# Layer 2 up to its MLP on whole float32 weights, attended beside the choice of tokens

## What is computed

```
x = _layernorm(x + attention(x, Wq, Wk, Wv, Wo))        # band: |block_i - block_j| <= 2, blocks of 64
scores = x @ w_router;  idx = sort(top_k(scores, 128))   # for each batch
sel = x[b, idx];  h = rms_norm(sel, ln1_w)
q, k, v = h @ wq + bq, h @ wk + bk, h @ wv + bv          # then rotary on q and k
att = softmax(causal(q @ k.T / sqrt(128)))               # over the chosen tokens of both batches
x1 = sel + (att @ v) @ wo
processed = x1 + (silu(rms_norm(x1, ln2_w) @ w_gate) * (rms_norm(x1, ln2_w) @ w_up)) @ w_down
gated = sigmoid(sel_scores) * processed + (1 - sigmoid(sel_scores)) * sel
x = _layernorm(x + x.at[b, idx].set(gated))
```

## Time and profile before

| What | Value |
|---|---|
| Median of three runs | 1432.89 us (1432.02 to 1435.05) |
| The profiled execution's own time | 1435.52 us |
| Its span, first to last instruction | 1433.5 us |
| TensorE, VectorE, ScalarE, GpSimd busy | 1286.4, 905.2, 606.8, 313.4 us |
| Instructions in the span | 19759 |
| Mean granted clock of TensorE | 0.953 of 2.4 GHz |
| Moved by DMA | 89.61 MB |

### The profile page before, as it was taken

One profiled execution on the slowest core, in us unless ns is written; L12 is line 12 of the kernel. 1 busy time (PEld: TensorE's weight loads), 2 busy tenths in 40 slices (PEclk: granted clock), 3 DMA queues, 4 the chain that ended last, 5 costly groups with the idle time before them and its releaser, 6 DMA issues.

```text
span 1433.5 us, 19759 instructions
## 1 busy us (share of the span) xinstructions
PE 1286.4 (90%) x7624; PEld 1145.9 (80%) x7624; DVE 905.2 (63%) x2328; ACT 606.8 (42%) x1388; POOL 313.4 (22%) x221
## 2 busy tenths in 40 slices
PE   6999999999999999999999999999998733767795
PEld 5898989889898988877879898989886633666795
DVE  4556565665565565787866556565556787686465
ACT  4444444444444444333434444444444222435352
POOL 2101120202020111231211021111202462252374
PEclk9999999999999999999999999999998876798798
DMA  5100110101010110133101010101100443253262
GB/s 172 35 22 30 31 44 30 45 16 45 15 45 30 45 65 10 64 99 118 45 26 45 15 45 26 34 30 40 40 33 1 161 147 96 77 170 124 75 207 101
DMA packets 70846, 89.61 MB, mean 63 GB/s; under 512 B 3360, under 2 KB 52512, under 8 KB 70752
## 3 DMA queue, kind: packets, MB, share of 16 engines
q1 hardware_dynamic: 70336, 87.04, 18.7%
q0 software_dynamic: 416, 1.31, 0.3%
HBM read 79.43 MB, written 8.91 MB: 62 GB/s over the span
## 4 chain that ended last, share of the span: by engine, by line
PE 67%; DVE 21%; ACT 7%; issue 3%; DMA 1%; POOL 0%; SPq 0%; ACTq 0%; DVEq 0%; POOLq 0%
PE proj L759 33%; PE y L759 10%; PE s L759 9%; PE o L759 8%; DVE arena L1179 8%; ACT arena L1020 4%; PE tp L831 4%; ACT prob L1054 2%; DVE prob L1214 2%; DVE work L1296 2%; DVE work L1388 1%; DVE yacc L1248 1%; ACT prob L1126 1%; DVE bn_out L1261 1%; DVE work L1391 1%
## 5 line engine op out<-in xcount | busy, mean ns | idle before, releaser
L759 PE MATMUL proj<-arena 128*128 128x256 f32 (+1 forms) x3552 | 649.3, 334 | 11.7 <-DVE arena L1179 7.5
L759 PEld LDWEIGHTS proj<-arena 128*128 128x128 f32 x3552 | 547.6, 192 | 74.1 <-DVE arena L1179 9.6
L1509 POOL TENSOR_TENSOR arena<-wraw,arena 128x1024 fp32r<-128x1024 f32 x98 | 242.8, 2487 | 936.0 <-ACT arena L1020 936.0
L1054 ACT ACTIVATE prob<-prob,stat 128x384 f32<-128x384 f32 (+1 forms) x256 | 151.0, 590 | 499.6 <-DVE stat L1214 499.6
L1179 DVE TENSOR_TENSOR arena<-proj,arena 128x512 fp32r<-128x512 f32 (+1 forms) x282 | 159.1, 569 | 314.1 <-ACT arena L1020 312.8
L759 PE MATMUL o<-arena 128*128 128x256 f32 (+1 forms) x1248 | 255.1, 333 | 8.8 <-DVE arena L1179 5.8
L759 PE MATMUL s<-arena 128*128 128x384 f32 (+3 forms) x1008 | 224.4, 340 | 10.8 <-DVE arena L1179 10.8
L759 PE MATMUL y<-arena 128*128 128x512 f32 (+1 forms) x888 | 214.7, 379 | 8.4 <-DVE stat L1419 4.4
L759 PEld LDWEIGHTS s<-arena 128*128 128x128 f32 x1008 | 175.2, 195 | 30.8 <-DVE arena L1179 15.7
L759 PEld LDWEIGHTS o<-arena 128*128 128x128 f32 x1248 | 185.8, 199 | 15.0 <-DVE arena L1179 7.7
L1179 DVE TENSOR_TENSOR arena<-tp,arena 128x384 fp32r<-128x384 f32 (+2 forms) x273 | 142.4, 522 | 83.5 <-ACT arena L1020 83.0
(11 more groups left out here) (136 smaller groups left out, 565.2 us busy)
## 6 DMA issues: line engine op xcount, KB each, us to landing
wraw<-in_L_attn_Wq SPq DMA_DIRECT2D x16, 512.0 KB, 3.3
wraw<-in_L_attn_Wk SPq DMA_DIRECT2D x16, 512.0 KB, 3.3
wraw<-in_L_attn_Wv SPq DMA_DIRECT2D x16, 512.0 KB, 3.3
wraw<-in_L_attn_Wo SPq DMA_DIRECT2D x16, 512.0 KB, 3.7
wraw<-in_L_ffn_wq SPq DMA_DIRECT2D x16, 512.0 KB, 5.1
yacc<-in_L_attn_hidden_states SPq DMA_DIRECT2D x16, 256.0 KB, 3.0
y_dram<-yacc SPq DMA_DIRECT2D x16, 256.0 KB, 3.2
out<-work SPq DMA_DIRECT2D x16, 256.0 KB, 2.1
```

Source lines behind the costliest of these rows:

```text
L759: ins = e.matmul(out_ap, l[a], r[b], start=first and i == 0 and j == 0, stop=final and i == n - 1 and j == 2, skip_group_check=skip)
L1054: e.activation(prob[s][:, 0:n], prob[s][:, 0:n], ACT.Exp, bias=stat[:, 4 * s + 1:4 * s + 2], scale=-1.0, accum_out=stat[:, 4 * s + 2:4 * s ...
L1509: e.tensor_tensor(lo, wraw[n % RAW_SLOTS][:], hi.bitcast(F32), ALU.subtract).then_inc(*G_.inc("wsplit", n, "lo"))
```

## The change

- **Whole products.** From the normed rows of layer 2 to the product with wo there are no halves: `one_pass` multiplies float32 tiles as they are. Weights wq, wk, wv and wo go by DMA into eight "homes" of 512 KB in the space of layer 1's transposed input, and no engine splits them. ScalarE copies each result from PSUM once (`whole_copy`).
- **Bias.** The eight bias rows are loaded once, split into halves on 40 partitions, and added by one fast product of 512 columns a block (`unit_row`, `ub`).
- **Rotation.** Sine, cosine and sum are VectorE's, read from PSUM; GpSimd's part is gone. The scaling of probabilities and both norm rows move from VectorE to ScalarE, with `shift` computed on GpSimd.
- **Last head of layer 1.** Its output is split tile by tile (`ot`) and not in halves of 512, and its output projection begins three ticks earlier.
- **Ranking in quarters.** `rows`, `count` and `tie` run for two tiles at a time, as soon as these are normed; `rank` adds six columns of counts.
- **Order.** Steps of layer 2 are tagged; each tick runs them in the order of `FLOW`. A pair of heads starts when its q, k and v blocks are there, so pairs of batch 0 stand among the comparisons of batch 1. The product with wo, the residual and the norm are done for each batch by itself.
- **End.** The gate is applied before the MLP, and after the last product one step takes the place of four; both batches' roots come before both rows.

```diff
+        def one_pass(e, out_ap, pairs, first, final, skip=False):
+            n = len(pairs)
+            for i, (l, r) in enumerate(pairs):
+                ins = e.matmul(out_ap, l, r, start=first and i == 0, stop=final and i == n - 1, skip_group_check=skip)
...
-                    ins = three_passes(e, bank[to][:, half * GW:(half + 1) * GW],
-                                       [([hT[0][:, k, :], hT[1][:, k, :]], [w4[0][:, k, :], w4[1][:, k, :]])
-                                        for k in range(KT)], half == 0, half == 1, skip=True)
+                    pe.wait_ge(*landed("p2", b, n, half))
+                    ins = one_pass(e, to, [(hT[:, 2 * half + k, :], w2[:, k, :]) for k in range(2)], half == 0, False, skip=True)
                     if half == 1:
-                        ins.then_inc(*T_.inc("p2", b, n, "made"))
+                        pe.wait_ge(*V_.at("ubias", "lo"))
+                        row = BIAS_AT[which] + c
+                        ins = e.matmul(to, spread(unit_row[:, row:row + 1], P), ub, start=False, stop=True,
+                                       skip_group_check=True)
...
+                elif kind == "ubias":
+                    act.wait_ge(*T_.at("out", NB * NG - 2, TT - 1, "made"))
+                    act.wait_ge(*V_.at("ubias", "zero"))
+                    act.wait_ge(*bias_loaded.all())
+                    hi_part(ub, work[1][0:BIAS_ROWS, :], "ubias")
...
+                elif kind == "lnorm":
+                    act.wait_ge(*G_.at("ln", b, t, "shift"))
+                    e.activation(row, row, ACT.Identity, bias=shift[i][:], scale=rstd[i][:]).then_inc(*S_.inc("lnorm", b, t, "row"))
...
+                    act.wait_ge(*V_.at("an2", b, n, "recip"))
+                    for h in range(2):
+                        of_head = prob[s][:, h * nk:(h + 1) * nk]
+                        ins = e.activation(of_head, of_head, ACT.Copy, scale=rc[:, h:h + 1])
...
-            if 0 <= u - END < TT:
-                project_out(NB * NG - 1, u - END)
-                running.append(finish_layer1(NB - 1, u - END))
+            for t in range(TT):
+                if u == END - 4 + t and t < TT - 1:
+                    job("ot", t)
+                if u == END - 3 + min(t, TT - 2):
+                    project_out(NB * NG - 1, t)
+                    running.append([finish_layer1(NB - 1, t), None])
...
+        FLOW = {None: 0, "choose": 0.5, "res": 0.7, "resh": 0.8, "o2": 1, "av2": 2, "at2": 3, "an2": 4, "as2": 5, "p2t": 6,
+                "p2r": 7, "p2": 8}
+        def tick(*later):
+            for entry in sorted(running, key=lambda entry: FLOW[entry[1]]):
+                if entry[1] in later:
+                    continue
+                entry[1] = next(entry[0], running)
+                if entry[1] is running:
+                    running.remove(entry)
...
+            if front and not any(entry[1] == "p2" for entry in running) and front[0][0] in h_there:
+                begin(project2(*front.pop(0)))
...
+                    sp.wait_ge(*T_.at(*emptied_by[n]))
+                    src = homely[n][1]
+                    e.dma_start(home[home_of[n]].rearrange("p (k n) -> p k n", k=src.shape[1]), src
+                                ).then_inc(home_loaded[home_of[n]].sem, 16)
...
-                    after(e.tensor_tensor(x1, bank[f"s{b}"][:, :], x1, ALU.add), "fin", b, "mlp")
-                    after(e.tensor_scalar(x1, x1, g[:, 1:2], None, ALU.mult), "fin", b, "gated")
-                    after(e.scalar_tensor_tensor(x1, x_sel[b][:], g[:, 2:3], x1, ALU.mult, ALU.add), "fin", b, "mixed")
-                    after(e.tensor_tensor(x1, x1, x_sel[b][:], ALU.add), "fin", b, "sum")
-                    after(e.bn_stats(bn_out[b][:], x1), "fin", b, "stats")
+                    after(e.scalar_tensor_tensor(y1, bank[f"s{b}"][:, :], gate[:, 4 * b + 1:4 * b + 2], y1, ALU.mult, ALU.add),
+                          "fin", b, "sum")
+                    after(e.bn_stats(bn_out[b][:], y1), "fin", b, "stats")
```

841 lines of the change are left out of this document (459 added, 382 removed).

## The result

Four executions of the changed kernel took 1372.25 to 1374.06 us, median **1373.0**; four of the kernel before beside them 1432.02 to 1435.09, median 1433.97. The ratio is 0.958, with a 95% interval from 0.956 to 0.959. The forecast was 1374. The profiled execution took 1373.61 us with a span of 1371.9.

What follows compares the result with a forecast made beforehand. Between layer 1 and the MLP, TensorE idled behind VectorE, ScalarE and weight splits; after the change TensorE binds. 1094.8 + 45 + 60 + 89 + 6.5 + 71 + 8 = 1374.3 us of span; median 1374, whole range 1338 to 1410.

Steps and rivals of the forecast that it cites:

- Layer 1, "nothing": Before 1094.8 us: norm rows moved from VectorE to ScalarE lie beside TensorE's busy slices, so no time changes.
- Stretch 1: From layer 1's last head at tile 4 to its last output product: 45 us (was 67.6), including a 5 us bias-load wait.
- Stretch 2: From there to batch 1's transposed rows: 60 us (was 66.7), with TensorE binding where VectorE did.
- The 4 us for the gather, root and norm: In stretch 2: a TensorE wait of 4 us for these steps, which stand behind the find.
- Stretch 3: From batch 1's transposed rows to the last product with wo: 89 us (was 109.5), 68 up to the last projection.
- The drain: End of stretch 3: last query block rotated, turned, attended and projected, 21 us with 16.2 of TensorE work.
- The price of a whole product: Float32 products in layer 2: 0.916 us for 512 columns, taken as four passes of 0.229.
- the first rival: Whole products cost only what transposes do, 0.44 us; chains bind stretches 2 and 3 at 45 and 66: 1336 us, chance 0.13.
- The stages queue: Rival: TensorE's steps each wait for ScalarE or loads, clock stays 0.77, 10 us more waits: 1406 us, chance 0.25.
- Half clock: Rival: gaps keep TensorE at 1.2 GHz through all three stretches: 1470 us, slower by 37, chance 0.05.
- The choice alone: Rival: the choice of tokens binds, stretches 2 and 3 last as before, only stretch 1 and end save: 1405 us, chance 0.07.
- The end: Behind the last MLP product: 8 us (was 14.3), from fewer steps, no queue behind the root, first start 1.4 us earlier.

Runs made afterwards that it cites:

- turn0: rin_early with batch 1's rotated blocks transposed one tick earlier: 1370.72 us, 13.4 more than rin_early.
- v_last: rin_early with the last two column blocks of layer 2 exchanged, last queries before last values: 1365.89 us, 8.6 more than rin_early.
- both: The changed kernel with the bias rows' load issued eight ticks earlier and batch 0's places found one tick later: 1360.96 us.
- rin_early: On top of both: batch 0's gathered rows get router score, squares and root five ticks earlier: 1357.27 us.
- old_end: The changed kernel with gate and mixing again behind the last product and batch 0's row written before batch 1's sum: 1375.42 us.

## Why the prediction came out right

TensorE sets stretches 2 and 3 as forecast, a whole product costs nearly what was put, and those two stretches save 34.7 us of the 61. That the total is met within 2.4 us of span is luck beyond that: the errors below go up to 10 us and cancel.

*Layer 1, "nothing".* Wrong by 3.6 us, the sum of three larger terms. The norm rows do not lie beside other work. VectorE, which wrote them itself before, now waits about 2.1 us for each of batch 0's eight until ScalarE has written it, and the ticks there take 6.8 us more. No run undoes this move alone, so the cause is argued, from the delay that grows tick by tick where the norms stand. The choice of batch 0, which is inside layer 1 too, was changed, and I costed only its second copy. Its comparisons win 9.7 us. Its find loses 6.3, where TensorE's queue reaches it before VectorE has written the places: 3.0 us idle, the rest at a lower clock. Finding a tick later takes nearly all of that away.

*Stretch 1, 45 us with a wait of 5 (0 to 10).* The mechanism and its place were right, the size was not: 9.55 us for ScalarE, near the upper end, and TensorE's loss was larger than the wait, 16.80 us, since the chain behind it (score, squares, root, stretched scaling) had not been set behind the load in the sum. Even the landing near 1108 that the sum gives hides two errors: the weight loads started at 1095.4 and not 1088, and moved mostly at 350 to 420 GB/s and not 207. The ticks were put too dear by 5.2 us, nearly as much as the first part was put too cheap. The runs show both halves: without the bias wait the stretch is 38.6 us, with the chain taken out too 36.0 (1093.8 to 1129.8).

*Stretch 2, 60 us.* 60.0, with TensorE busy for 51.5 of it where 51.6 was put, and idle for 8.5 where 9 was put; the clock is 0.94 where 0.9 was put, so the work is some 2 us more than counted. The first wait was where it was put, 4.0 us for the first rotations. The 4 us for the gather, root and norm did not come: TensorE does not stand before the transposes at 1205.19. Smaller gaps, the longest 1.9 us, took their place. The text says that this stretch buys batch 0's pairs. Held back, they cost about 4 us, so they bought little; the quarters, which I had weighed only as narrower comparisons, bought 14. The term was right and its two parts were credited wrongly.

*Stretch 3, 89 us.* 7.5 too much. Up to the last projection at 1264.4 it takes 59.2 us where 68 were put. TensorE is busy for 56.8 of it at clock 1.00, where 56.3 us of work became 62.6 by a clock of 0.9: 5.8 us. Its idle time there is 2.4 us where 5 were put. The drain was put at 21 and is 22.3.

*The price of a whole product.* 0.916 put, 0.86 measured, 6% off; the first rival, 0.44 as by the transposes, falls, also by the doubled products. The Trainium skill (FP8 and Floating Point Precision, TensorE Precision Notes) has four passes for true FP32; by it, with 0.229 a pass, the price would be 0.916, and the trace, at 0.86, is close to it. What the first rival said of the chains was right only in the sum: with products at about half its price the two stretches take 51.0 and 58.3 us, 109.3 together, where it had 45 and 66. No run has its 0.44.

*The stages queue* did not come: TensorE idles for 6 us of stretch 3, and the clock stayed up. But turn0 and v_last show how near it is. One tick less between a rotation and its transposes costs 13.4 us. *Half clock* did not come either: the three stretches have 0.82, 0.94 and 0.98. *The choice alone* sets stretch 2 when the pairs are taken away, at 47.6 us, and when the quarters are, at 72.2; in the change as made it does not.

*The end*, 8 put and 9.4 measured; the moved steps and the queue behind the root, to which I gave most of the 6.3 us, are worth 2.9 by the run, and the first sum waits for a norm row of ScalarE.

## What to carry to other kernels

A small load that an in-order engine waits for belongs ahead of the large ones, by issue, and the chain that hangs on it should be pulled as early as its inputs allow: here that and a find one tick later gave 1357.3 us against 1373.0, ratios 0.949 and 0.958, with none of the work changed. A step given to an engine with time to spare still costs if the engine that gave it away needs the result at once: eight norm rows moved so stand at 6.8 us in layer 1. When work is moved beside a chain, ask which engine sets that stretch: pairs moved from one TensorE-bound stretch to another bought 4 us, a head start for the chain itself 14. And where the program issues by ticks, try one tick more between a producer and TensorE: here one such tick was worth 3 to 6 us at the find and 13 at the transposes.

## What the runs showed of the hardware

**Some VectorE steps are held until a GpSimd instruction ends.** Two kinds of step that meet GpSimd's weight splits are not slowed in proportion but end just after a split: the scaling of batch 0's rows takes 2.84 us instead of 0.75 (the changed kernel and both), and the scaling of probabilities 2.38 instead of 0.42 (rin_early). One split alone takes GpSimd 2.4 us. Steps of VectorE that read PSUM take their usual 0.56 during the same splits. The Trainium skill (SBUF — State Buffer, SBUF: two separate sides) calls the ports that the two share an exclusive lock, held for a whole instruction, with the loser blocked, and names as VectorE's steps that take it those with two inputs in SBUF or in a 2-port mode; by it such a step costs the rest of the split it meets and then its own time. The rows agree to 0.2 us: 1101.24 + 2.38 = 1103.62 against 1103.82, the splits' end at 1103.40 and 0.42 more.

**The price of a stall is the clock behind it, and it varies.** Seven kernels with the same code up to there have the same 3.0 us stall near 800 us and spend 20.5 to 23.2 us on the same four tiles, against 17.5 without the stall. In the changed kernel 5 us at a granted clock of 0.50 follow it, in old_end none. The Trainium skill (TensorE: Matmul & The Clock Gate, HAM oscillation — how this bites in real kernels) says that gaps bring the lower clock back; six of the seven traces agree, old_end's does not, and the six differ in how long the lower clock lasts.

**A whole float32 product shows as two records** of about 0.43 us each for 512 columns; the order of instructions has one. Taking one record for a whole product would halve the price.
